# ScalarE issues the transfer of the rows of maxima itself, one transfer a half, in place of three on the sync engine

## The chip, the cores and the metric

The kernel runs on one core of one Trainium2 chip. The metric is device time in microseconds of one execution; the median of three runs is given. The profile is of one further execution. Engines are named TensorE (PE), VectorE (DVE), ScalarE (ACT), GpSimd (POOL) and the sync engine (SP), which only issues transfers.

## The reference

Two layers in sequence on `x` (16 sequences of 256 tokens, 256 features), each with a residual connection, both with 16 heads of 16 features:

```python
def layer0(x, t):                       # t: the condition, 16 x 64
    x1 = x + attention(tc_rmsnorm(x, t, g1, b1), Wq, Wk, Wv, Wo)      # softmax(q k / 4) v, no mask
    return x1 + swiglu(tc_rmsnorm(x1, t, g2, b2), gate_w, hid_w, out_w)   # hidden width 1024
x = x + layer0(x, cond_256)

def layer1(x, mask, c):
    scores = where(mask, -inf, q @ k.T / 4)          # one mask of 256 x 256 for all
    out = (softmax(scores) @ v) @ Wo.T
    xn = out / sqrt(mean(out * out) + 1e-6) * rms_scale
    shift, sc = split(silu(c) @ Wc.T + bc)
    return xn * (1 + sc) + shift
x = x + layer1(x, mask, cond_256)
```

The softmax needs the maximum of each row of scores. The kernel subtracts it by appending it, in three bf16 parts that add up to the f32 value, as three more rows of the operand that holds q (against rows of ones in the operand of k), so that a matmul gives scores minus maximum.

## The kernel before

The work is a pipeline over 32 sequence passes (16 sequences of layer 0, then 16 of layer 1). In step `s0` (from -3 to 33) each engine works on several passes at once: normalization of pass s+3 ("N"), q and k projections of s+2 ("A"), values and the first scores of s+1 ("V", "B1"), the second scores, exponentials and weighted sums of s ("B2"), the division and output projection of s-1 ("C"), and the feed-forward network of s-2 and s-3 ("C2", "C3") or the result of s-2 ("R"). Each step has eight slots `g`, one for two heads, and every engine's program is written out in its own order, slot by slot. Steps 3 to 12 and 19 to 28 are loops of two steps a turn, in which waits compare with registers. Nothing schedules: engines run their lists and meet at semaphores.

The maxima go through the engines twice in a step, once for each half of eight heads. TensorE's first scores (`s1ps`, L568 or L583) are reduced by VectorE to `nmax` (L875, L882); GpSimd splits them in three parts (`nparts`, L1247 to L1253); TensorE transposes the parts into a bank (`work` or `acc`, L726); ScalarE copies the bank to the buffer `rows`, 24 partitions by 256 (`shift_store`, L1092); SP moves `rows` into three partitions of the q operand `qst` (`rows_in`, L469). TensorE's second scores (`s2ps`, L606) of heads 0 and 8 wait for the landing (`shift_loaded`). The second half (heads 8 to 15) is handled in slot 1 of the step that uses it in slot 4; the first half is handled in slot 5 (from step 19 on at the head of slot 6 on ScalarE) and is used in slot 0 of the next step.

SP's list in a step: load x; `rows_in(1)`; write the parts `qp` of q and then `kp` of k to a scratch buffer in HBM (L412, two transfers each); after these have landed, `read_stack` of the first half (L422, three transfers of 384, 256 and 128 KB from scratch to the operands `stack`); in layer 1 store the result (L427); `rows_in(0)`; `read_stack` of the second half.

Names on ScalarE: `exps` (L1055, s2ps to `E`), `tanh` of feed-forward block i (L1073, bank F{i} to `th`), `h_high_part` (L1079, `hh`), `store_oT` (L1065), `query_high` (L1097) and the copy of k (L1146) that round the projections to bf16 in `qp` and `kp`, `middle` (L1102) that rounds VectorE's rest (L919) once more, and the copy `oh` (L1115), whose rest `ol` VectorE makes (L909) for the output projection on TensorE (L525 to L527 with `oh`, `ol`). `dg` (L945) are VectorE's diagonals of inverse roots, which TensorE broadcasts (L718). Two banks `work0`, `work1` are used in turn by all projections, so a bank is opened when its earlier use is read.

Of the kernel before, what the change touches and what calls it, by code (L numbers as in the profile page):

```python
# [58 lines left out]
MASKED = PARTS + 1  # L59
ROWS = MASKED + 3  # L60
SLOTS = 8
UNITS = 16
# [131 lines left out]
def after(eng, sem, count):  # L194

    if isinstance(count, int) and count <= 0:
        return
    eng.wait_ge(sem, count)
# [31 lines left out]
def build(nc, xT, w0, w_ffn, w_out, w1, condT, cond_w, cond_b, rms_scale, mask, maskT, yT):  # L230
    ctx = ExitStack()
    with ctx:
# [18 lines left out]
        qst = [t[:, 0, :, :] for t in stack]  # L251
# [36 lines left out]
        rows = sb("rows", [P, T], BF16)  # L288
# [94 lines left out]
        def _(sp):  # L383
# [53 lines left out]
            def step(st):  # L437
# [18 lines left out]

                rows_used = [held(UNITS * n_b2), held(UNITS * (n_b2 - 1))]
                rows_made = [None, None]
                for half_, stage in enumerate(("B1", "B2")):
                    if L[stage] is not None:  # L460
                        b, k = st.bank(f"sh{half_}")
                        rows_made[half_] = (work_free[b], held(k + 1))
                result_made = held(st.n(-2 - B) + 1)

                def rows_in(half_):
                    after(sp, s2_full, rows_used[half_])
                    after(sp, *rows_made[half_])
                    for r in range(3):
                        sp.dma_start(qst[par if half_ else 1 - par][MASKED + r:MASKED + r + 1, 8 * half_:8 * half_ + 8, :],  # L469
                                     rows[8 * r:8 * r + 8, :]).then_inc(shift_loaded[half_], 16)  # L470

# [14 lines left out]
                load_swap(4)  # L486
                if L["B2"] is not None:
                    rows_in(1)
                if L["A"] is not None:
# [13 lines left out]
                if L["R"] is not None:  # L503
                    store_result(st.n(-2 - B), result_made)
                if L["B1"] is not None:
                    rows_in(0)
                if L["A"] is not None:
# [12 lines left out]
        def _(pe):  # L520
# [67 lines left out]
            def scores(st, g):  # L588
                n, par = st.n(0), st.par
                if g in (0, 4):  # L590
                    after(pe, shift_loaded[g // 4], 48 * (n + 1))
                short = st.L["B2"] == 1 and not st.full
# [436 lines left out]
        def _(act):  # L1029
# [59 lines left out]
            def shift_store(st, half_):  # L1089
                bank, free = opened(st, f"sh{half_}")  # L1090
                after(act, shift_loaded[1 - half_], 48 * (st.n(0) + half_))
                a.copy(nT, bank[0:24, 0:P].bitcast(BF16)).then_inc(free, 1)  # L1092

            def query_high(st):
# [284 lines left out]
```

## Time and profile before

| | |
|---|---|
| median of 3 runs | 1008.09 us (1007.32 to 1013.06) |
| the profiled execution | 1008.46 us, of which the span from first to last instruction is 1006.6 us |
| mean granted TensorE clock | 0.967 of full |
| busy: PE, DVE, ACT, POOL | 90%, 57%, 54%, 41% |
| transfers | 91.29 MB, mean 91 GB/s |
| a steady step of layer 0 / of layer 1 | about 39.6 us / 17.4 us |

The span is 1.9 us shorter than the execution's own time. In the rows, an engine line gives start, duration, engine, line, operation, output and input, and in brackets the idle time just before it and what ended that; SPq is SP's queue, whose instructions are the issues and not the transfers' time. A queue can stand idle at no cost, and only what TensorE waits for reaches the end.

### The profile page before, as it was taken

Reading aid. Unit: us, or ns where it says so; the run is one execution under the profiler, and the core shown is the slowest. Engines: PE = TensorE matmul, PEld = TensorE weight load, DVE = VectorE, ACT = ScalarE, POOL = GpSimd, SP = SyncE. Lnnn points to the kernel's source line nnn. Section 1 sums busy time; section 2 is a strip of 40 time slices with the busy share of each in tenths; the row PEclk is TensorE's granted clock in tenths of the full one; section 3 lists DMA queues with packets and bytes.
Section 4 is the critical chain, followed back from the end, with each engine's and each line's share of the span. In section 5 each row is a group of like instructions: output and inputs, shape, how many; then the busy total and the mean of one; then the engine's idle time right before and its main releaser. Section 6 shows DMA issues by size and latency. Waiting matters only on the chain.

```text
span 1006.6 us, 24326 instructions
## 1 busy us (share of the span) xinstructions
PE 909.2 (90%) x8188; PEld 780.6 (78%) x8188; DVE 570.3 (57%) x1104; ACT 547.5 (54%) x1130; POOL 415.2 (41%) x633
## 2 busy tenths in 40 slices
PE   3578899999999999999999999999999789888874
PEld 3456698898888988988889889889887677777653
DVE  3366556557555565575565756545455455555541
ACT  2246556546455565464554665554556566666652
POOL 5223344443443444434334344344444454444522
PEclk9779999999999999999999999999999999999997
DMA  6555423322332233223322242232437576576611
GB/s 204 110 106 122 91 64 75 75 65 59 66 86 42 63 73 73 63 58 68 84 42 63 69 91 65 65 76 66 94 74 167 119 160 147 142 166 144 157 36 34
DMA packets 83070, 91.29 MB, mean 91 GB/s; under 512 B 7776, under 2 KB 70016, under 8 KB 83008
## 3 DMA queue, kind: packets, MB, share of 16 engines
q1 hardware_dynamic: 83008, 90.50, 39.8%
q8 instruction: 35, 0.57, 0.3%
q14 instruction: 27, 0.22, 0.1%
HBM read 60.30 MB, written 29.36 MB: 89 GB/s over the span
## 4 chain that ended last, share of the span: by engine, by line
PE 73%; issue 8%; DVE 7%; ACT 5%; POOL 3%; DMA 1%; SPq 1%; POOLq 0%; DVEq 0%; ACTq 0%
PE work L525 11%; PE work L527 11%; PE work L526 11%; PE pvps L622 8%; PE s2ps L606 7%; PE s1ps L583 5%; PE work L710 4%; PE acc L525 3%; PE acc L526 2%; PE acc L527 2%; PE work L656 2%; PE s1ps L568 2%; PE work L718 1%; DVE rest L919 1%; DVE th L959 1%
## 5 line engine op out<-in xcount | busy, mean ns | idle before, releaser
L1055 ACT ACTIVATE E<-s2ps 128x512 f32<-128x512 f32 x384 | 214.1, 596 | 184.2 <-PE s2ps L606 110.8
L882 DVE TENSOR_REDUCE nmax<-s1ps 128x2 f32<-128x512 f32 x256 | 163.9, 682 | 32.1 <-PE s1ps L583 31.9
L525 PE MATMUL work<-xch,Gh 128*128 128x256 f32 x512 | 154.5, 302 | 0.0
L959 DVE SCALAR_TENSOR_TENSOR th<-th,work 128x256 f32<-128x256 f32 x128 | 53.8, 420 | 168.7 <-ACT th L1073 168.7
L1328 POOL TENSOR_TENSOR hl<-hf,hh 128x256 fp32r<-128x256 f32 x128 | 94.9, 742 | 131.0 <-PE acc L527 77.3
L526 PE MATMUL work<-xcl,Gh 128*128 128x256 f32 x512 | 147.1, 287 | 0.0
L527 PE MATMUL work<-xch,Gl 128*128 128x256 f32 x512 | 146.9, 287 | 0.0
L606 PE MATMUL s2ps<-stack 100*128 100x256 bf16 x768 | 127.7, 275 | 2.1 <-DMA stack<-rows 2.0
L875 DVE TENSOR_REDUCE nmax<-s1ps 128x4 f32<-128x512 f32 x128 | 85.6, 685 | 36.5 <-PE s1ps L568 36.4
L525 PEld LDWEIGHTS work<-xch,Gh 128*128 128x128 f32 x512 | 99.3, 194 | 8.2 <-issue 6.6
L622 PE MATMUL pvps<-E,vaug 128*32 128x256 f32 x1536 | 97.5, 387 | 6.3 <-ACT E L1055 4.0
L1233 POOL TENSOR_TENSOR qp<-rest,qp 128x512 bf16<-128x512 f32 x32 | 37.2, 1163 | 156.3 <-ACT qp L1102 156.3
L527 PEld LDWEIGHTS work<-xch,Gl 128*128 128x128 f32 x512 | 100.0, 195 | 0.0
L526 PEld LDWEIGHTS work<-xcl,Gh 128*128 128x128 f32 x512 | 99.9, 195 | 0.0
L583 PE MATMUL s1ps<-stack 96*128 96x256 bf16 x512 | 81.9, 281 | 9.4 <-DMA stack<-scr 4.9
L1073 ACT ACTIVATE th<-work 128x256 f32<-128x256 f32 x128 | 49.1, 384 | 72.3 <-PE work L527 72.3
L525 PE MATMUL work<-xnh,Wh 128*128 128x256 f32 x256 | 79.3, 310 | 1.4 <-issue 0.8
L606 PEld LDWEIGHTS s2ps<-stack 100*128 100x128 bf16 x768 | 67.3, 98 | 14.1 <-issue 2.3
L622 PEld LDWEIGHTS pvps<-E,vaug 128*32 128x32 f32 x1536 | 43.8, 110 | 40.3 <-issue 9.5
L525 PE MATMUL acc<-hh,Uh 128*128 128x256 f32 x256 | 74.2, 290 | 0.2
L526 PE MATMUL work<-xnl,Wh 128*128 128x256 f32 x256 | 74.4, 291 | 0.0
L527 PE MATMUL work<-xnh,Wl 128*128 128x256 f32 x256 | 74.2, 290 | 0.0
(131 smaller groups left out, 2149.1 us busy)
## 6 DMA issues: line engine op xcount, KB each, us to landing
stack<-scr SPq DMA_DIRECT2D x64, 384.0 KB, 4.6
stack<-scr SPq DMA_DIRECT2D x64, 256.0 KB, 5.2
scr<-qp SPq DMA_DIRECT2D x64, 192.0 KB, 2.3
scr<-kp SPq DMA_DIRECT2D x64, 192.0 KB, 2.3
stack<-scr SPq DMA_DIRECT2D x64, 128.0 KB, 5.6
X<-xT SPq DMA_DIRECT2D x16, 256.0 KB, 4.5
yT<-crm SPq DMA_DIRECT2D x16, 256.0 KB, 5.2
stack<-rows SPq DMA_DIRECT2D x196, 4.0 KB
```

The source lines that it names most:

```text
L525: mm(out, lh, rh, start=first, stop=False, skip_group_check=True)
L526: mm(out, lh, rl, start=False, stop=False, skip_group_check=True)
L527: return mm(out, ll, rh, start=False, stop=last, skip_group_check=True)
L583: last = mm(bank[:, T * i:T * (i + 1)], qst[par][0:PARTS, h, P * qh:P * (qh + 1)], kst[par][0:PARTS, h, :], start=st.L["B1"] == 0, stop=Tr ...
L606: last = mm(bank[:, T * i:T * (i + 1)], kst[par][0:ROWS, h, P * kh:P * (kh + 1)], qst[par][0:ROWS, h, :], start=not add_mask, stop=True, s ...
L622: last = mm(pvps[32 * i:32 * (i + 1), T * (j % 2):T * (j % 2 + 1)], v_of[:, kh, h, :], E[:, exp_slot(layer, st.full, h // 2, kh), T * (h % ...
L875: v.tensor_reduce(nmax[:, g // 4, :, 2 * (g % 4):2 * (g % 4) + 2], s1ps[g % 2][:, :].rearrange("p (q h t) -> p q h t", q=2, h=2), AX_X, AL ...
L882: v.tensor_reduce(nmax[:, g // 4, qh, 2 * (g % 4):2 * (g % 4) + 2], s1ps[u % 2][:, :].rearrange("p (h t) -> p h t", h=2), AX_X, ALU.max, n ...
L959: v.scalar_tensor_tensor(th[:, i % 2, :], th[:, i % 2, :], 1.0, bank[:, 0:T], ALU.add, ALU.mult).then_inc(silu_ready, 1)
L1055: a.activation(E[:, exp_slot(st.L["B2"], st.full, g, kh), :], s2ps[g % 2 if short else u % 2][:, :], ACT.Exp, scale=SCORE_SCALE).then_inc( ...
L1073: a.activation(th[:, i % 2, :], bank[:, 0:T], ACT.Tanh, scale=0.5).then_inc(tanh_ready, 1)
L1328: p.tensor_tensor(hl[:, i % 2, :], hf[:, i % 2, :], hh[:, i % 2, :].bitcast(F32), ALU.subtract).then_inc(h_low, 1)
```

## The change

`rows_in` and its counts leave SP's program. ScalarE's `shift_store` now issues one transfer from the 24 partitions of `rows` to all three partitions of `qst`, behind its own copy: it waits that the scores which last used those heads are done (`s2_full`) and that its own copy is done (`work_free[b]`). The semaphore `shift_loaded` then counts 16 a half in place of 48, and the two waits on it, on TensorE and on ScalarE, follow. Layer, data and all other orders stay.

```diff
--- before.py
+++ after.py
@@ -454,20 +454,7 @@
-                rows_used = [held(UNITS * n_b2), held(UNITS * (n_b2 - 1))]
-                rows_made = [None, None]
-                for half_, stage in enumerate(("B1", "B2")):
-                    if L[stage] is not None:
-                        b, k = st.bank(f"sh{half_}")
-                        rows_made[half_] = (work_free[b], held(k + 1))
                 result_made = held(st.n(-2 - B) + 1)
-
-                def rows_in(half_):
-                    after(sp, s2_full, rows_used[half_])
-                    after(sp, *rows_made[half_])
-                    for r in range(3):
-                        sp.dma_start(qst[par if half_ else 1 - par][MASKED + r:MASKED + r + 1, 8 * half_:8 * half_ + 8, :],
-                                     rows[8 * r:8 * r + 8, :]).then_inc(shift_loaded[half_], 16)
@@ -484,8 +471,6 @@
-                if L["B2"] is not None:
-                    rows_in(1)
@@ -502,8 +487,6 @@
-                if L["B1"] is not None:
-                    rows_in(0)
@@ -588,7 +571,7 @@
-                    after(pe, shift_loaded[g // 4], 48 * (n + 1))
+                    after(pe, shift_loaded[g // 4], 16 * (n + 1))
@@ -1088,8 +1071,14 @@
                 bank, free = opened(st, f"sh{half_}")
-                after(act, shift_loaded[1 - half_], 48 * (st.n(0) + half_))
+                after(act, shift_loaded[1 - half_], 16 * (st.n(0) + half_))
                 a.copy(nT, bank[0:24, 0:P].bitcast(BF16)).then_inc(free, 1)
+
+                b, k = st.bank(f"sh{half_}")
+                after(act, s2_full, UNITS * (st.n(0) - half_))
+                after(act, work_free[b], k + 1)
+                act.dma_start(qst[st.par if half_ else 1 - st.par][MASKED:ROWS, 8 * half_:8 * half_ + 8, :],
+                              nT).then_inc(shift_loaded[half_], 16)
```

ScalarE's list in slot 5 of a layer 0 step (`rows` is the copy of the maxima, `th` the tanh of block 5, `hh` the cast of block 4's h; the names in brackets are the semaphores that the instruction waits for). Before:

```order
88 L1065 COPY oT<-pvps 128x512 [waits work_full1,work_full0,pv_done]
89 L1092 COPY rows<-work 24x256 [waits shift_loaded1,work_full1]
90 L1073 ACTIVATE th<-work 128x256 [waits work_free0,work_full0]
91 L1079 CAST hh<-hf 128x256 [waits down_done,work_free1]
92 L1055 ACTIVATE E<-s2ps 128x512 [waits pv_done,s2_full] x2
```

And in the changed kernel:

```order
94 L1048 COPY oT<-pvps 128x512 [waits work_full1,work_full0,pv_done]
95 L1075 COPY rows<-work 24x256 [waits shift_loaded1,work_full1]
96 L1080 DMA stack<-rows 3x8x256 [waits work_free1,s2_full]
97 L1056 ACTIVATE th<-work 128x256 [waits work_free0,work_full0]
98 L1062 CAST hh<-hf 128x256 [waits down_done,work_free1]
99 L1038 ACTIVATE E<-s2ps 128x512 [waits pv_done,s2_full] x2
```

One issue stands between the copy and the tanh; nothing else moved.

ScalarE's list in slot 1 of a layer 1 step (`kp` first the copy and then the middle part of k). Before:

```order
519 L1092 COPY rows<-acc 24x256 [waits shift_loaded0]
520 L198 REGISTER_ALU
521 L1146 CAST kp<-work 128x512 [waits k_written,work_full1]
522 L1102 CAST kp<-rest 128x512 [waits work_free1]
523 L198 REGISTER_ALU
```

And in the changed kernel:

```order
542 L1075 COPY rows<-acc 24x256 [waits shift_loaded0]
543 L198 REGISTER_ALU
544 L1080 DMA stack<-rows 3x8x256 [waits work_free2,s2_full]
545 L198 REGISTER_ALU
546 L1135 CAST kp<-work 128x512 [waits k_written,work_full1]
547 L1091 CAST kp<-rest 128x512 [waits work_free1]
```

Here the issue and one more register operation stand ahead of k's copy. SP's list loses its three transfers a half, 32 steps long, and keeps its other transfers in their order.

## Rows read from the trace of the kernel before

**Rows 1.** The page, its first part: busy time of each engine.

```profile
PE 909.2 (90%) x8188; PEld 780.6 (78%) x8188; DVE 570.3 (57%) x1104; ACT 547.5 (54%) x1130; POOL 415.2 (41%) x633
```

**Rows 2.** Waits of SP's queue: total us, times, longest.

```profile
SPq L198 <- ACT rows L1092: 349.3, 59, 10.6
```

**Rows 3.** Issues on SP: minimum, median and maximum duration in ns.

```profile
L469 SPq DMA_DIRECT2D stack<-rows x192: 634/640/794, 60.0 to 977.8; - x192
...
L422 SPq DMA_DIRECT2D stack<-scr x192: 308/427/1412, 38.2 to 955.1; - x192
```

**Rows 4.** TensorE's waits from 690 to 985 us, which holds layer 1.

```profile
PE work L525 <- DVE ol L909: 19.1, 13, 1.6
...
PE s2ps L606 <- DMA stack<-rows: 2.0, 3, 1.5
```

**Rows 5.** Timeline of one layer 1 step, SP's issues and TensorE.

```profile
791.96 2.07 SPq L469 DMA_DIRECT2D stack<-rows  x3
...
796.57 0.40 PE L568 MATMUL s1ps<-stack 97*128 97x128 bf16 x4 [1.24 <-DMA stack<-scr]
...
798.44 0.39 PE L606 MATMUL s2ps<-stack 100*128 100x256 bf16 x2 [1.48 <-DMA stack<-rows]
```

**Rows 6.** Timeline of slots 5 and 6 of a layer 0 step.

```profile
387.87 0.36 ACT L1092 COPY rows<-work 24x256 bf16<-24x256 bf16 x1
388.13 0.38 ACT L1073 ACTIVATE th<-work 128x256 f32<-128x256 f32 x1
...
388.54 0.42 DVE L959 SCALAR_TENSOR_TENSOR th<-th,work 128x256 f32<-128x256 f32 x1 [1.26 <-ACT th L1073]
...
390.53 0.68 DVE L945 TENSOR_TENSOR dg<-ident,rstd 128x512 f32<-128x512 f32 x1
...
391.54 0.42 DVE L959 SCALAR_TENSOR_TENSOR th<-th,work 128x256 f32<-128x256 f32 x1 [0.33 <-ACT th L1073]
391.64 0.60 PE L718 MATMUL work<-dg,ones 128*128 128x256 f32 x2
...
392.47 0.70 PE L718 MATMUL work<-dg,ones 128*128 128x256 f32 x2 [0.23 <-DVE hf L963]
```

**Rows 7.** Timeline of slots 1 to 3 of a layer 1 step.

```profile
834.80 1.16 POOL L1233 TENSOR_TENSOR qp<-rest,qp 128x512 bf16<-128x512 f32 x1 [2.08 <-ACT qp L1102]
...
836.03 0.34 ACT L1092 COPY rows<-acc 24x256 bf16<-24x256 bf16 x1
...
836.45 2.02 SPq L469 DMA_DIRECT2D stack<-rows  x3
...
836.93 0.59 ACT L1146 CAST kp<-work 128x512 bf16<-128x512 f32 x1 [0.55 <-PE work L527]
...
839.47 0.69 DVE L909 TENSOR_TENSOR ol<-work,oh 128x512 fp32r<-128x512 f32 x1 [1.17 <-ACT oh L1115]
...
840.21 0.39 PE L525 MATMUL work<-oh,Wh 128*128 128x256 f32 x1 [1.56 <-DVE ol L909]
```

**Rows 8.** Timeline, what stands behind the copy of the rows in other steps.

```profile
267.38 0.38 ACT L1073 ACTIVATE th<-work 128x256 f32<-128x256 f32 x1 [1.00 <-PE work L527]
...
365.76 0.59 ACT L1097 CAST qp<-work 128x512 bf16<-128x512 f32 x1 [0.41 <-PE work L527]
...
592.20 0.41 DVE L945 TENSOR_TENSOR dg<-ident,rstd 128x256 f32<-128x256 f32 x1
593.25 0.60 PE L718 MATMUL work<-dg,ones 128*128 128x256 f32 x2
...
764.29 0.59 ACT L1146 CAST kp<-work 128x512 bf16<-128x512 f32 x1 [0.55 <-PE work L527]
...
847.47 1.09 ACT L1055 ACTIVATE E<-s2ps 128x512 f32<-128x512 f32 x2 [1.06 <-PE s2ps L606]
```

**Rows 9.** Chain of waits, ScalarE's queue between two instructions: start, us, what.

```profile
838.54 0.06 issue
838.60 0.04 ACTq L198
```

## The prediction

> **What bounds the kernel now.** I read the page first. TensorE is busy 90% of the span and the other engines 41% to 57% [rows 1], so a transfer or a wait counts only where TensorE stands behind it. The waits of SP's queue come next, because the change is made there: SP stands 349.3 us at the rows of maxima [rows 2]. That figure is no price. It is idle time of a queue, and I ask who waits for SP. TensorE's own waits answer: over the whole of layer 1 it lost 2.0 us in three waits to the landed rows, against 19.1 us in thirteen waits to the low half of the attention output (`ol`) [rows 4]. So the removed stand is nearly free already, and the question is what the step costs on ScalarE, where the 19.1 us chain begins.
>
> **What is removed.** Per half SP issues three transfers; 192 of them lasted 640 ns each at the median [rows 3], so SP gets back 192 x 0.64 = 123 us of issuing. What stands behind them on SP: behind the second half's rows, the writes of qp; behind the first half's, the second half of the stack load. In layer 0 the qp write waits for GpSimd anyway, and the stack load for TensorE's scores. In layer 1 the write of qp could start some 2.5 us earlier (GpSimd has the low part ready at 834.80 + 1.16 = 835.96, while SP is still to issue until 838.5), but the stack load needs kp as well, whose write is issued after GpSimd's later kp part [rows 7]. So the stack load does not move: 0. The second half's load moves up by under 1 us and is wanted half a step later: 0.
>
> What can be gained is the late landing. In one step the rows were issued at 791.96, behind the first half of the stack and the result's store on SP's queue, and TensorE waited 1.48 us for them at 798.44, after 1.24 us for the stack itself [rows 5]. The other two waits of the kind make up 0.5 us. A transfer issued by ScalarE starts earlier and does not stand in SP's queue. I count all three waits, 2.0 us [rows 4], as gained, and leave the 1.24 us.
>
> At this place the Trainium skill speaks both ways. "DMA: Bandwidth & Descriptors", section "Queues, rings and completion order", says that a DMA engine takes turns between the queue rows that have work, packet by packet, so the rows on ScalarE's own row would pass the backlog; by that, 2.0 us come back, as I count. Its section "Issuing engines are not separate DMA queues" says that transfers of all engines interleave on the same sixteen engines and that only issuing time is saved; by that the waits would partly stay and the sum be up to 2 us higher. No row of before has a transfer on ScalarE's queue.
>
> **What is added: 64 issues on ScalarE.** Each stands behind ScalarE's own copy (0.34 to 0.36 us [rows 6, 7]) and must see it finished, where the next instruction now starts while the copy still drains. No row shows an issue on ScalarE. The nearest rows are SP's: 640 ns for one row of the same data, 427 ns for a stack transfer of up to 384 KB [rows 3]. The time does not follow bytes or pieces, so I take 0.64 us for the one transfer of three rows, with 0.43 below, zero as the far lower end, and three times 0.65 = 1.95 us as the upper end, if it costs what its three parts did. Around it: 0.08 us from the copy's end to the issue (836.03 + 0.34 to SP's issue at 836.45 [rows 7]) and about 0.2 us for two queued waits of the next instruction, at 0.06 + 0.04 us each [rows 9].
>
> The Trainium skill has a price that would make all this vanish: "DMA: Bandwidth & Descriptors", section "Anatomy of one DMA", lists about 50 ns for a sequencer's dispatch. The 640 ns rows of SP contradict it for the issuing queue, and I go by the rows; with 50 ns the sum would be the gain alone, 1006.1.
>
> *Layer 0, slot 5.* Here `tanh` of block 5 stands directly behind the copy of the rows: copy at 387.87, tanh at 388.13 [rows 6]. Now: copy ends 388.23, + 0.08 + 0.64 + 0.2 = 389.15, 1.02 us later. VectorE's product starts from it at 388.54 and runs without idle time through two maxima to the diagonals, which end at 390.53 + 0.68 = 391.21; TensorE takes them at 391.64 [rows 6]. Of the 0.43 us between, 0.06 is the signal; 0.37 us is cover. 1.02 - 0.37 = 0.65 us come through. The second broadcast at 392.47 moves as much, because VectorE's next product (391.54, idle 0.33 before it) falls behind the diagonals. Six steps of the trace look so (their copies start at 147, 187, 226, 348, 388 and 427 us; the fifth stands for them): 6 x 0.65 = 3.9. Two more, the one shown and the next, have shorter diagonals: 592.20 + 0.41 = 592.61 against 593.25 leaves 0.58 of cover, 0.44 come through [rows 8], 0.9 together. In the other loop steps TensorE reaches the place later and tanh already waits 1.0 us for it [rows 8]: 0. The cast of h behind the tanh moves along; GpSimd and the down projection that read it come late enough by my reading: 0.
>
> *Layer 0, slot 1.* The next instruction, the copy of qp, waits 0.41 us for TensorE now [rows 8] and would start about 0.5 us later. The bank that it shares with VectorE is wanted again after about that time: I take 0, and 0.1 us in each of 13 steps as the bound.
>
> *Layer 1, slot 1.* The rows' copy ends at 836.37. kp's copy starts at 836.93, when TensorE is through [rows 7]. Now 836.37 + 0.08 + 0.64 + 0.2 = 837.29, so 0.36 us late, and everything behind it is the chain at which TensorE waits: kp's rest on VectorE, its middle part and `oh` on ScalarE, `ol` on VectorE (839.47), TensorE at 840.21 after 1.56 us idle [rows 7]. No cover at all. Eleven steps look so, the first at 764.29 [rows 8], the last at 942.59: 11 x 0.36 = 4.0.
>
> *Layer 1, slot 6.* The exponentials behind the copy wait 1.06 us for TensorE [rows 8]; 0.08 + 0.64 + 0.2 = 0.92 fits: 0.
>
> **Sum.** 3.9 + 0.9 + 4.0 - 2.0 = +6.8 us on the profiled 1008.46, which lies 0.4 above the median of 1008.09: 1014.9 on the median. I take **1015.0**. With 0.43 us an issue: 6 x 0.44 + 2 x 0.23 + 11 x 0.15 - 2.0 = +2.8, 1010.8; with 0.85 us, +10.8, 1018.9. Every other cost of ScalarE's is between zero and (c) below.
>
> **Rivals.**
> (a) *The issue is nearly free on ScalarE.* At up to 0.2 us all covers hold and the gain of 2.0 us is left: 1006. For it: nothing on ScalarE was measured. Against: SP's rows never fall below 308 ns.
> (b) *Two issuers collide (slower).* SP no longer stands at the rows, so in layer 1 it issues the two qp writes at about 836.03 and holds until 836.95, exactly when ScalarE wants to issue (836.45). If one must wait for the other, kp's chain loses 0.5 us more: 11 x 0.5 = 5.5, together 1020.4. It decides where SP's pair begins before ScalarE's copy ends, in every step of that kind. Against: layer 0 has the two apart. The Trainium skill's "Perfetto Trace Analysis", section on the HWDGE DMA instruction, describes a lock that an issuer waits for, on a descriptor generator shared by two sequencers; no run here shows it yet.
> (c) *One transfer costs what its three parts did.* With 1.95 us, each term grows by 1.31: 6 x 1.96 + 2 x 1.75 + 11 x 1.67 - 2.0 = +31.6, 1039.7, and slot 6 of layer 1 loses its cover too. Against: the stack rows, whose many pieces cost 427 ns.
> (d) *More is gained than the waits show.* The step of rows 5 may be late because of SP's queue as a whole, and its 1.24 us go too; with a free issue as in (a) that is 1008.1 - 2.0 - 1.2 = 1004.9, and any shorter standing in eleven steps may add a little: about 1003. A gain of over 1% has no row.
>
> **How the numbers follow.** Forecast 0.50, (a) 0.20, (b) 0.17, (c) 0.06, (d) 0.07. One per cent, 10 us, is about what a measurement of this kernel tells from no change. The forecast with its bounds spans 1010.8 to 1018.9. The range reaches over (a) and (b), with room in (b) for a somewhat longer issue: 1004 to 1025. Slower by over 1% (above 1018.2): all of (c), nearly all of (b) and the top of the forecast, 0.29. Faster by over 1%: 0.06. Within: 0.65.
>
> **What will show it.** ScalarE's queue has 64 issues; their length decides nearly all. In layer 0's slot 5 the tanh starts about 1.3 us behind the start of the rows' copy instead of 0.26, and TensorE gets a new wait for the diagonals, about 0.6 us, six times. In layer 1 the wait for `ol` grows from 1.6 to 1.9 us, and the waits for landed rows go. SP's longest waits turn to GpSimd's qp. I am wrong if the issue on ScalarE is not near 0.64 us, if SP's issues and ScalarE's stretch one another, or if the intervals of lower granted clock in layer 0, each worth more than a microsecond, fall on other slots.

## The result and the profile after

The changed kernel took 1032.79 us (median of 4 runs, 1030.51 to 1034.88) against 1010.58 us (4 runs, 1007.32 to 1014.01) for the kernel before on the same chip: ratio 1.0194, 95% interval [1.0158, 1.0229]. It is slower, and 8 us above the upper end of the range. The profiled execution took 1030.51 us, its span is 1028.6 us, the granted clock 0.954 of full speed on average. The line numbers of the changed kernel are 17 lower on TensorE, VectorE and in most of ScalarE's code (L508 for L525, L892 for L909, L1075 for L1092) and 11 lower for what stands behind the issue in the program (L1135 for L1146, L1086 for L1097, L1222 for L1233). The issue on ScalarE is L1080.

The page of the changed kernel, busy time of each engine (against [rows 1]):

```profile
PE 923.3 (90%) x8188; PEld 788.1 (77%) x8188; DVE 572.3 (56%) x1104; ACT 547.3 (53%) x1130; POOL 416.1 (40%) x633
```

The same 8188 matmuls kept TensorE busy 14.1 us longer, and its idle time (span less busy) went from 1006.6 - 909.2 = 97.4 to 1028.6 - 923.3 = 105.3 us. So 8 us of the difference between the two profiles are waits and 14 us are matmuls that ran slower.

The issues on ScalarE: minimum, median and maximum in ns, first and last start.

```profile
L1080 ACTq DMA_DIRECT2D stack<-rows x64: 728/733/1346, 58.0 to 997.4; - x64
```

Timeline of the changed kernel, slots 5 and 6 of a layer 0 step (against [rows 6]):

```profile
192.25 0.36 ACT L1075 COPY rows<-work 24x256 bf16<-24x256 bf16 x1
192.70 0.73 ACTq L1080 DMA_DIRECT2D stack<-rows  x1
193.60 0.38 ACT L1056 ACTIVATE th<-work 128x256 f32<-128x256 f32 x1 [0.99 <-ACT rows L1075]
...
196.84 1.40 PE L701 MATMUL work<-dg,ones 128*128 128x256 f32 x4 [0.65 <-DVE dg L928]
```

From the copy's end (192.61) to the issue are 0.09 us, the issue takes 0.73, and 0.17 us behind it the tanh starts: 1.35 us behind the start of the copy, where it was 0.26. TensorE has a wait for the diagonals that was not there, 0.65 us.

Slot 1 of layer 0 (against the 0.41 us in [rows 8]), and slot 1 of layer 1 with the chain behind it (against [rows 7]), both from the timeline:

```profile
169.15 0.35 ACT L1075 COPY rows<-work 24x256 bf16<-24x256 bf16 x1
169.59 0.77 ACTq L1080 DMA_DIRECT2D stack<-rows  x1
170.47 0.58 ACT L1086 CAST qp<-work 128x512 bf16<-128x512 f32 x1 [0.97 <-PE work L510]
...
855.57 0.35 ACT L1075 COPY rows<-acc 24x256 bf16<-24x256 bf16 x1
856.00 0.73 ACTq L1080 DMA_DIRECT2D stack<-rows  x1
856.89 0.58 ACT L1135 CAST kp<-work 128x512 bf16<-128x512 f32 x1 [0.98 <-PE work L510]
...
859.42 0.69 DVE L892 TENSOR_TENSOR ol<-work,oh 128x512 fp32r<-128x512 f32 x1 [1.17 <-ACT oh L1104]
860.17 0.39 PE L508 MATMUL work<-oh,Wh 128*128 128x256 f32 x1 [1.98 <-DVE ol L892]
```

The name behind the arrow can mislead: k's copy "waits 0.98 us for PE", but what ran out last is ScalarE's own issue, 856.00 + 0.73 = 856.73. The copy of k starts 1.32 us behind the start of the copy of the rows, against 0.90 before, and TensorE waits 1.98 instead of 1.56 us.

Waits of the changed kernel, TensorE and then SP's queue (us in total, times, longest; in the kernel before, over the whole program, `ol` had 20.6 us in 14, the diagonals 15.6 us in 5):

```profile
PE work L508 <- DVE ol L892: 25.2, 14, 2.1
PE work L701 <- DVE dg L928: 20.1, 13, 5.7
...
PE s2ps L589 <- DMA stack<-rows: 3.4, 3, 2.2
```

```profile
SPq L422 <- PE s2ps L589: 269.5, 28, 17.0
SPq L198 <- POOL qp L1222: 235.7, 26, 15.9
```

SP's stand at the rows [rows 2] is gone and turned into others, as forecast. But the waits for landed rows did not go: 3.4 us against 2.0 [rows 4]. The longest stands where layer 1's maxima meet the first full pair of stack loads:

```profile
771.46 0.73 ACTq L1080 DMA_DIRECT2D stack<-rows  x1
...
771.69 1.48 SPq L422 DMA_DIRECT2D stack<-scr  x3
...
777.13 0.39 PE L589 MATMUL s2ps<-stack 100*128 100x256 bf16 x2 [2.21 <-DMA stack<-rows]
```

SP no longer stands at the rows, so it issues the second half of the stack load (768 KB) 0.23 us behind the start of ScalarE's issue. In the trace's record of packets the 24 packets of the rows begin at 774.56, 3.1 us behind the start of the issue, and end at 775.44; TensorE goes on at 777.1. In the kernel before the three transfers of the rows were issued at 757.50 to 759.51, ahead of the stack load at 759.55, and TensorE waited 0.27 us at 760.76.

**Where the time went, by stretches.** The borders are starts of the same copies of the rows in both kernels; columns: stretch, its length, busy time of the engines (with counts of instructions), granted clock, share of the DMA engines, GB/s. Before:

```profile
0.00:124.45 124.45, 81.74 (x588) 62.54 (x589) 65.19 (x114) 52.77 (x91) 46.03 (x71) 0.89 0.54 128
124.45:589.47 465.02, 458.80 (x4114) 409.98 (x4113) 284.63 (x540) 253.35 (x556) 192.97 (x278) 0.98 0.31 67
589.47:757.07 167.60, 163.95 (x1524) 146.22 (x1523) 91.99 (x191) 92.69 (x204) 71.53 (x109) 1.00 0.34 76
757.07:773.41 16.34, 14.23 (x144) 11.32 (x142) 9.68 (x19) 11.51 (x24) 7.44 (x14) 1.00 0.67 149
773.41:951.67 178.26, 155.38 (x1543) 125.97 (x1542) 100.12 (x200) 114.95 (x220) 83.48 (x140) 0.99 0.66 149
951.67:1006.60 54.93, 35.15 (x286) 24.61 (x285) 18.68 (x40) 22.20 (x43) 13.79 (x23) 0.83 0.19 48
```

After:

```profile
0.00:128.68 128.68, 86.92 (x588) 64.34 (x589) 66.49 (x114) 53.07 (x91) 46.01 (x71) 0.83 0.51 124
128.68:600.72 472.04, 462.35 (x4114) 410.88 (x4113) 285.35 (x540) 253.84 (x556) 194.40 (x278) 0.98 0.29 66
600.72:771.01 170.29, 165.25 (x1524) 146.58 (x1523) 91.78 (x191) 92.53 (x205) 71.47 (x109) 1.00 0.33 75
771.01:791.54 20.53, 15.77 (x143) 12.51 (x142) 9.87 (x19) 11.39 (x24) 7.33 (x14) 0.92 0.50 113
791.54:975.09 183.55, 159.39 (x1543) 130.44 (x1543) 100.11 (x200) 114.40 (x221) 83.14 (x140) 0.96 0.64 145
975.09:1028.60 53.51, 33.60 (x286) 23.37 (x285) 18.69 (x40) 22.09 (x43) 13.71 (x23) 0.85 0.20 49
```

Longer by 4.2 us at the start, 7.0 in layer 0, 2.7 on the way to layer 1, 4.2 in the one step of the late landing, 5.3 in layer 1, and 1.4 shorter at the end: 22.0. At the start TensorE does not wait longer (124.45 - 81.74 = 42.7 us idle before, 41.8 after); the same 588 matmuls take 86.92 instead of 81.74 us, at a clock of 0.83 instead of 0.89. In layer 1 the granted clock is 0.96 against 0.99. In detail, three equal stretches of one step of the changed kernel:

```profile
838.80:842.20 3.40, 1.34 (x13) 1.06 (x11) 2.16 (x4) 1.84 (x4) 1.16 (x1) 1.00 0.07 19
842.20:845.60 3.40, 3.40 (x19) 3.40 (x17) 0.95 (x3) 1.93 (x4) 2.35 (x3) 0.51 0.58 158
845.60:849.00 3.40, 3.40 (x42) 2.22 (x42) 1.38 (x2) 2.90 (x6) 1.96 (x5) 0.99 1.03 190
```

In the first TensorE is idle 2.06 us, waiting for `ol`; in the second it is busy throughout at half the clock (0.51, which is 1.2 of 2.4 GHz) and gets 19 matmuls begun, against 42 in the third.

**The base moved too.** The kernel before was run again beside the experiments. 74 of these runs have a median of 1013.9 us (1005.7 to 1023.5), with granted clocks of 0.946 to 0.967; time and clock go together (correlation -0.8). Two more, of 1062.9 and 2187.1 us, lie far outside and are left out here and below. The 1008.09 us and the profile that I started from, at 0.967, are the fast edge of that. So the change costs 17 to 19 us of 1014 (16.8 us on the one chip where both kernels were run again), and the 14 us of slower matmuls between the two profiles are in part this luck.

### The profile page after: what moved, and what is told of

The parts are those of the page before. It is cut to its first block, busy times and chain, and to the rows that moved or that the text cites. A ratio compares the mean times of both kernels' runs of the same rounds, so it can differ in the third digit from the quotient of the medians.

```text
span 1028.6 us, 24173 instructions
## 1 busy us (share of the span) xinstructions
PE 923.3 (90%) x8188; PEld 788.1 (77%) x8188; DVE 572.3 (56%) x1104; ACT 547.3 (53%) x1130; POOL 416.1 (40%) x633
## 4 chain that ended last, share of the span: by engine, by line
PE 64%; issue 12%; DVE 8%; ACT 7%; POOL 4%; ACTq 2%; DMA 2%; POOLq 0%; SPq 0%; DVEq 0%
PE work L508 10%; PE work L509 9%; PE work L510 9%; PE pvps L605 8%; PE s2ps L589 6%; PE s1ps L566 5%; PE work L693 4%; PE work L639 2%; PE acc L508 2%; PE work L701 2%; PE acc L509 2%; PE acc L510 2%; ACTq L1080 2%; DVE nmax L865 2%; DMA stack<-rows 1%
## 5 line engine op out<-in xcount | busy, mean ns | idle before, releaser
L508 PE MATMUL work<-xch,Gh 128*128 128x256 f32 x512 | 155.1, 303 | 0.1
L508 PEld LDWEIGHTS work<-xch,Gh 128*128 128x128 f32 x512 | 99.8, 195 | 8.5 <-issue 6.6
L1222 POOL TENSOR_TENSOR qp<-rest,qp 128x512 bf16<-128x512 f32 x32 | 37.1, 1160 | 158.8 <-ACT qp L1091 158.8
L508 PE MATMUL work<-xnh,Wh 128*128 128x256 f32 x256 | 79.2, 309 | 1.8 <-issue 0.7
L1222 POOL TENSOR_TENSOR kp<-rest,kp 128x512 bf16<-128x512 f32 x32 | 37.2, 1161 | 95.5 <-ACT kp L1091 95.5
L508 PE MATMUL acc<-hh,Uh 128*128 128x256 f32 x256 | 73.9, 289 | 0.3
```

The source lines that it names most:

```text
L508: mm(out, lh, rh, start=first, stop=False, skip_group_check=True)
L1222: p.tensor_tensor(parts[:, lo_at, :, :], rest[:, :, :], parts[:, 1, :, :], ALU.subtract).then_inc(low, 1)
```

## The experiments

TensorE's idle time is span less busy time of the profiled execution. The kernel before had medians of 1014.2 us beside `sp_one`, the two halves and `act_late` (one chip), 1014.4 us beside `act_pad`, `changed_again` and the first two fillings (a second chip), and on a third chip 1012.6 us beside `act_wait`, `act_from3`, `act_three` and `sp_one_fill` and 1013.3 us beside the two holds and `act_fill0`. Times from different chips are best compared by their distance from these. What is called an interval of lower clock below is a short stretch in which TensorE runs at about half its clock.

### One transfer, still on SP

```diff
-                    for r in range(3):
-                        sp.dma_start(qst[par if half_ else 1 - par][MASKED + r:MASKED + r + 1, 8 * half_:8 * half_ + 8, :],
-                                     rows[8 * r:8 * r + 8, :]).then_inc(shift_loaded[half_], 16)
+                    sp.dma_start(qst[par if half_ else 1 - par][MASKED:ROWS, 8 * half_:8 * half_ + 8, :],
+                                 nT).then_inc(shift_loaded[half_], 16)
```

> The kernel before, but SP issues the three rows as one transfer (24 partitions to 3) in its old places; ScalarE issues nothing. Theory A (the cost is ScalarE's issue: 0.73 us and the wait for its own copy, 64 times, ahead of work that TensorE waits for, and the lower granted clock that follows TensorE's longer idle times): as before within 0.4%, no new wait of TensorE for the diagonals, wait for ol at 1.6 us, SP gets back 1.3 us a half. Theory B (the merged transfer lands later than three small ones): slower than before by 0.3% or more, with waits for stack<-rows at the 3.4 us of the changed kernel or above.

1010.76 us, ratio 0.9973 [0.9946, 0.9999]; TensorE idle 91.6 us. Waits of TensorE, and the issue in the timeline at the switch to layer 1:

```profile
PE work L524 <- DVE ol L908: 20.2, 14, 1.6
PE work L717 <- DVE dg L944: 14.6, 5, 5.7
...
PE s2ps L605 <- DMA stack<-rows: 0.6, 1, 0.6
```

```profile
762.53 0.73 SPq L468 DMA_DIRECT2D stack<-rows  x1
763.30 1.36 SPq L422 DMA_DIRECT2D stack<-scr  x3
```

The gain that I counted exists, 1.4 of the 2.0 us of waits for rows and nearly 6 us of idle time in all, but it belongs to the one transfer in place of three, not to the engine that issues it. And one transfer of three rows costs SP 0.73 us too: ScalarE issues neither faster nor slower.

### ScalarE issues one half only

Two kernels, on the base of the last: `act_half1` leaves the first half to SP and gives the second (slot 1) to ScalarE, `act_half0` the other way (slots 5 and 6).

```diff
                 a.copy(nT, bank[0:24, 0:P].bitcast(BF16)).then_inc(free, 1)
+                if not (half_ == 1):
+                    return
+                b, k = st.bank(f"sh{half_}")
+                after(act, s2_full, UNITS * (st.n(0) - half_))
+                after(act, work_free[b], k + 1)
+                act.dma_start(qst[st.par if half_ else 1 - st.par][MASKED:ROWS, 8 * half_:8 * half_ + 8, :],
+                              nT).then_inc(shift_loaded[half_], 16)
```

> Half of the change: ScalarE issues only the second half's rows (slot 1), SP the first half's as one transfer. Theory A: the wait for ol grows from 1.6 to about 2.0 us in eleven steps of layer 1 (+4.5 us) and TensorE is at half clock in some three or four more intervals there (+5 to 7 us); no new wait for the diagonals in layer 0. In all +7 to +14 us. Theory B (landing): under +3 us, because the second half's landing is not waited for.

> The other half of the change: ScalarE issues only the first half's rows (slot 5, slot 6 from step 19), SP the second half's as one transfer. Theory A: the new wait for the diagonals, 0.65 us in some seven steps of layer 0 and 0.4 in two more (+5 us), the wait for ol stays at 1.6 us, in all +5 to +10 us. Theory B: all of the change's loss (+20 us) is here, with waits for stack<-rows of 3 us or more in layer 1.

`act_half1`: 1013.12 us, ratio 0.9981 [0.9947, 1.0014], 2.4 us over the single transfer on SP, less than expected. Its waits are as expected, `ol` at 25.4 us, and its idle time is 98.4 us, 6.8 more; but its ten runs had the higher clock, 0.964 on average against 0.955. The stretches tell where, though no experiment tells why: between the copies that stand at 124.45 and 589.47 us in the kernel before (layer 0), `act_half1` took 461.60 us at a clock of 1.00 and the single transfer on SP 468.01 us at 0.97, while in layer 1 (773.41 to 951.67) it took 184.09 against 177.04 us. So layer 1 lost 7 us, the lower end of what was expected, and a layer 0 faster by 6.4 us hid most of it.

`act_half0`: 1023.3 us, ratio 1.0093 [1.0064, 1.0121], 12.5 us over it, a little more than expected. TensorE's waits:

```profile
PE work L717 <- DVE dg L944: 18.2, 10, 5.7
...
PE s2ps L605 <- DMA stack<-rows: 2.4, 1, 2.4
```

The new waits for diagonals and the late landing belong to the first half, the longer `ol` to the second.

### The issues at places where ScalarE waits anyway

The changed kernel with the issue in a function of its own, called later: the first half behind the cast of h in slot 6 (layer 1: as now), the second behind the exponentials of slot 3 (from step 19: 2).

```diff
+                    if g == (2 if st.s0 >= SPARE else 3) and L["B2"] is not None:
+                        shift_issue(st, 1)
...
+                    if g == 6 and st.s0 < SPARE and L["B1"] is not None:
+                        shift_issue(st, 0)
```

> ScalarE issues both halves' transfers as in the changed kernel, but at places where it stood idle in the trace: the first half's behind the cast of h in slot 6 (steps before 19) and as now in slot 6 (from step 19), the second half's behind the exponentials of slot 3 (slot 2 from step 19). Theory A: the loss goes, within 4 us of the kernel before; no wait for the diagonals, wait for ol at 1.6 us. Theory B or a theory that SP's freed queue disturbs the loads: as slow as the changed kernel, +15 us or more.

1017.53 us, ratio 1.0021 [0.9986, 1.0055], 3.3 us over the kernel before. `ol` is back at 20.6 us and the diagonals at 14.0, but TensorE waits 5.0 us in five waits for landed rows, the longest here in the timeline:

```profile
767.83 0.73 ACTq L1081 DMA_DIRECT2D stack<-rows  x1
768.07 1.47 SPq L422 DMA_DIRECT2D stack<-scr  x3
...
773.36 0.39 PE L589 MATMUL s2ps<-stack 100*128 100x256 bf16 x2 [2.53 <-DMA stack<-rows]
```

Sixty-four issues of 0.73 us on ScalarE cost nearly nothing where nobody waits behind them. The place is the price, not the issue.

### ScalarE held without a transfer

The kernel before; behind ScalarE's copy come the change's two waits and two copies that nobody reads.

```diff
+                for r in range(2):
+                    after(act, pad_done, 2 * (2 * st.n(0) + 2 - half_) + r)
+                    a.copy(rows[64:88, :].rearrange("p (r t) -> p r t", r=2),
+                           ones[64:88, :][:, None, :].to_broadcast([24, 2, P])).then_inc(pad_done, 1)
```

> The kernel before, with SP's three transfers as they were; ScalarE only gets, behind its copy of the rows, the two waits of the change and then two small copies in a row, which together hold it about as long as the issue did (estimated from the 0.26 us between two such instructions and the 0.36 us of one: about 0.7 to 0.8 us), and which nobody reads. It parts the time that ScalarE is held from the transfer itself. Theory A (the loss is ScalarE being held in front of tanh in layer 0 and in front of k's copy in layer 1, with the lower granted clock that follows): TensorE gets waits for the diagonals of about 0.6 us in six or seven steps of layer 0 and the wait for ol grows from 1.6 to about 2.0 us, though no transfer is on ScalarE's queue; the time is +12 to +22 us over before. Rival B (the transfer issued by ScalarE is what costs: later landing, descriptor work, another queue): the same waits would appear but the time stays within 6 us of before.

The changed kernel once more, as the base on this chip:

> The changed kernel once more, on the same chip as the next experiments, as their base. Both theories: 1.5 to 2.3% over before.

The two copies took 0.83 us together and the tanh of slot 5 started 1.38 us behind the copy of the rows (191.77, 193.15), as long as in the changed kernel. The padded kernel took 1028.81 us, ratio 1.0138 [1.0055, 1.0221], the changed one 1031.16 us, 1.0145 [1.0062, 1.0228]. Waits of the padded kernel:

```profile
PE work L526 <- DVE ol L910: 25.7, 14, 2.1
PE work L719 <- DVE dg L946: 21.6, 15, 5.7
```

Its idle time is 106.3 us against 105.9 in the changed kernel. So 14.5 of 16.8 us come without any transfer on ScalarE's queue; rival B falls. The other 2.3 us are not clear of the spread of four runs.

### ScalarE only waits

> The kernel before; ScalarE gets only the two waits of the change behind its copy of the rows (own copy done, scores done), and neither issue nor padding. SP keeps its transfers. By the rows the tanh of layer 0 then starts about 0.3 us later than before, which is less than the 0.37 us of cover in front of the diagonals, and k's copy of layer 1 (0.55 us of idle time in front of it) not later at all. Theory A: no new waits for diagonals, ol stays at 1.6 us, and the time is within 3 us of before. Rival B (to see its own copy finished is itself dear on ScalarE): 4 us and more over before.

```diff
+                b, k = st.bank(f"sh{half_}")
+                after(act, s2_full, UNITS * (st.n(0) - half_))
+                after(act, work_free[b], k + 1)
```

1015.54 us, ratio 1.0023 [0.9991, 1.0054], 2.9 us over the kernel before and not clear of it; `ol` 20.9 us in 14, diagonals 15.1 us in 5, idle 95.5 us. The tanh of slot 5 starts 0.59 us behind the start of the copy instead of 0.26 (189.53, 190.12). The cover of [rows 6], which is the slack between the diagonals' end and TensorE's use of them, takes the 0.3 us, as worked out.

### Matmuls that fill TensorE's wait

Twelve matmuls ahead of layer 1's output projection, into the bank that it overwrites, in the changed kernel (`act_fill`) and in the kernel before (`sp_fill`).

```diff
             def output_projection(st):
+                if st.s0 >= SPARE:
+                    bank, full = open_bank(st, "Wo")
+                    for _i in range(12):
+                        mm(bank[:, 0:D], Wh[:, 3, 0, 0:P], Wl[:, 3, 0, :], start=True, stop=True, skip_group_check=True)
```

> The changed kernel, and in layer 1 (from step 19) TensorE runs twelve matmuls of 128x256 ahead of the output projection into the bank that this will fill from its start, while it waits for ol; their result is overwritten. Theory A (the intervals of lower granted clock in layer 1 follow TensorE's idle time of about 2 us at ol): the intervals at 777, 804, 842, 896 and 951 us thin out to two or fewer, TensorE's busy time outside the added matmuls falls by several us, and the time is 3 to 8 us under the changed kernel, if the added matmuls fit into the wait. Rival B (the clock falls regardless of this idle time): as many intervals as before, and the time is the same or, where the matmuls outlast the wait, up to 5 us longer.

> The kernel before with the same twelve matmuls in front of the output projection in layer 1. Theory A: its wait there was 1.6 us, and only about two intervals of lower clock stood in layer 1, so 0 to 3 us faster than before. Rival B: unchanged, or up to 5 us slower since twelve matmuls may outlast a wait of 1.6 us.

`act_fill` took 1026.81 us, 4.3 us under the changed kernel on the same chip, although it does more work. Its timeline, and the stretch that answers to 791.54:975.09 above:

```profile
854.41 1.69 PE L673 MATMUL work<-Wl,Wh 128*128 128x256 f32 x12
...
856.27 0.39 PE L508 MATMUL work<-oh,Wh 128*128 128x256 f32 x1 [0.18 <-DVE ol L896]
```

```profile
790.41:968.97 178.56, 170.91 (x1663) 139.60 (x1663) 100.12 (x200) 114.53 (x221) 83.26 (x140) 1.00 0.66 148
```

`ol` comes no earlier, at 855.53, 3.87 us behind the start of the copy of the rows at 851.66 (without the filling 859.42 - 855.57 = 3.85), yet the stretch is 178.56 instead of 183.55 us, at a clock of 1.00 instead of 0.96. Here the clock followed TensorE's idle time (7.7 instead of 24.2 us in the stretch). `sp_fill` took 1011.73 us, 2.6 us under the kernel before, ratio 0.996 [0.9923, 0.9997], with a clock of 1.00 in layer 1 as well; it had less to win, as expected.

The same in layer 0, five matmuls ahead of the first broadcast of slot 6:

> The changed kernel, and in layer 0 from step 3 on TensorE runs five matmuls of 128x256 ahead of the first broadcast of slot 6, into the bank that this overwrites, while it waits 0.65 us for the diagonals. Theory A (what the change lost in layer 0 between 147 and 589 us is idle time alone, since both kernels have five intervals of lower clock there): as many intervals as without them and the time within 2 us of the changed kernel, since the diagonals come no earlier. Rival B (there too the clock follows the new idle time, as in layer 1): intervals go, and it is 2 to 6 us faster than the changed kernel.

1030.50 us, 0.7 under the changed kernel of the other chip, ratio 1.0171 [1.0117, 1.0225]. The diagonals' waits of 0.65 us are filled (17.4 us in 6 against 21.5 in 13), its profile has three intervals of lower clock in layer 0 where the changed kernel had five, and the time is the same within what can be told. In layer 0 the filling wins nothing: the diagonals come no earlier, and what they delay stays delayed. Idle time alone does not set the clock: in the layer 0 stretch named above, the single transfer on SP has 6.2 us of idle time at a clock of 0.97, and `act_half1` 7.0 us at 1.00.

### The first steps left to SP

```diff
+                if not (st.s0 >= 3):
+                    return
```

with SP's single transfer in steps below 3.

> The changed kernel, but in the first steps (up to step 2) SP still issues the one transfer a half; ScalarE issues from step 3 on. Between the kernels the copies of the rows had shifted by 4.6 us at 147 us already, which my sum has no term for. Theory A (that part comes from ScalarE being held in the start-up steps, where TensorE waits for it as well): 3 to 6 us under the changed kernel, about 1026. Rival B (the 4.6 us are the clock at the start, which varies from one execution to the next): within 2 us of the changed kernel.

1028.18 us, 3.0 under `changed_again` and 4.6 under the first measurement, on other chips; against the kernel before on its own chip it loses 15.6 us where `changed_again` loses 16.8, so the times tell nothing sure. In the trace the copy that stands at 124.45 us before starts at 124.29, where the changed kernel had 128.68. But this trace is of the fastest of the four runs, and kernels whose ScalarE issues nothing differ as much:

```profile
0.00:124.29 124.29, 81.79 (x588) 62.57 (x589) 65.55 (x114) 52.75 (x91) 45.95 (x71) 0.89 0.54 128
...
0.00:127.16 127.16, 86.63 (x588) 64.86 (x589) 66.43 (x114) 53.20 (x90) 46.05 (x71) 0.84 0.53 125
```

The first line is `act_from3`, the second `act_wait`. The same copy starts at 124.3 to 127.2 us in the six traces without an issue on ScalarE in the first steps (mean 125.6) and at 126.9 to 130.0 in the five with the whole change (mean 128.4). So rival B, the clock at the start, explains much of this, and a start-up part of the change is likely, 2.8 us by the means, but not shown. Whatever it is, it is matmuls at the lower clock and not waiting.

### Three transfers on ScalarE

The issue in a loop of three, one for each part.

> The changed kernel, but ScalarE issues three transfers a half, as SP did, so that it is held for three times 0.73 = 2.2 us instead of 0.73 us. Theory A (held time goes through once the cover is used up): 1.46 us more in some ten steps of layer 0 and eleven of layer 1, 31 us, and up to 10 us more at places that had cover until now: 30 to 45 us over the changed kernel, 1060 to 1075. Rival B (a fixed price for having the transfer on ScalarE's queue): under 10 us over the changed kernel.

1152.52 us, ratio 1.1371 [1.1327, 1.1416]: 121 us over the changed kernel (on another chip), three times the expected. One issue of one row is 627 ns, the three of a half hold ScalarE 1.96 us. TensorE is busy 979.2 us, 56 more, and idle 178.6, 73 more; its clock is 0.902. Its waits:

```profile
PE work L508 <- DVE ol L892: 36.4, 13, 3.3
PE work L701 <- DVE dg L928: 28.3, 18, 6.5
PE work L653 <- DVE rest L902: 21.1, 17, 1.9
PE s2ps L589 <- DMA stack<-rows: 17.1, 12, 3.0
```

Theory A had the direction and not the shape: the cost is no line through the two places where cover ran out. With 1.2 us more in a row, waits open that had none (k's rest, landed rows in twelve steps), and each longer idle time is followed by slower matmuls. My rival (c) worked out 1039.7 us for this hold with the same straight line.

### SP holds the stack load back until the rows have landed

```diff
+                rows_landed = held(16 * (n_b1 + 1))
...
+                    if L["B1"] is not None:
+                        after(sp, shift_loaded[0], rows_landed)
                     mask_row_in(st, 1)
                     read_stack(par, 1)
```

In the changed kernel (`stack_hold`) and in the one with late issues (`late_hold`).

> The changed kernel, and SP waits ahead of the second half of the stack load until ScalarE's transfer of the first half's rows has landed (it stood at their issue in the kernel before). Theory A (SP, no longer standing at the rows, issues the stack load in the same moment as ScalarE its rows, and the rows land behind it: issue at 771.46, stack load at 771.69, TensorE waits 2.21 us and a lower clock follows): the wait for landed rows in the step where layer 1's first scores begin goes from 2.2 us to under 0.5 us, its jump of 3.8 us between the copies of 757 and 763 us goes, and the time is 3 to 4 us under the changed kernel, about 1028. Rival B (a transfer on ScalarE's queue lands late by itself): the wait stays at about 2 us and the time within 2 us of the changed kernel.

> The kernel whose ScalarE issues later, at places where it waits anyway (1017.53 us, with 5.0 us of waits for landed rows), with the same hold on SP. Theory A: it loses most of those 5.0 us and comes to 1012 to 1014 us, level with the kernel before. Rival B: unchanged at 1017.

`stack_hold`: 1026.81 us, ratio 1.0138 [1.0084, 1.0191]. That is 4.4 us under the changed kernel on another chip, and by the distance from the kernel before 3.3 us (13.5 against 16.8). Its timeline:

```profile
771.48 0.73 ACTq L1083 DMA_DIRECT2D stack<-rows  x1
...
773.72 1.25 SPq L422 DMA_DIRECT2D stack<-scr  x3
```

No wait for landed rows is left on TensorE in layer 1, and from this copy to the next it takes 6.7 us, nearly as before (6.33), where the changed kernel took 10.1: 3.4 us in this one step. The rows issued at 771.48 were home by 773.7; their packets ran from 772.85 to 773.11, 1.4 us behind the start of the issue and not 3.1, and took 0.3 instead of 0.9 us. `late_hold`: 1012.78 us, ratio 1.0009 [0.9976, 1.0042], 4.7 less than without the hold (on another chip; 3.8 by the distances from the kernel before), and its waits for rows fell from 5.0 us in five to 1.5 us in three. So a transfer on ScalarE's queue does not land late by itself; it does when the stack load is issued beside it. In `sp_one` the rows, issued by SP 0.77 us ahead of the same load, have their first packet 1.4 us behind the issue as well (763.90). Whether a lead of 0.23 us would be enough on SP's own queue was not tried.

### The two good parts together

SP's single transfer, and the twelve matmuls.

> SP issues one transfer a half in the old places, and TensorE has the twelve matmuls ahead of the output projection in layer 1. The single transfer had a ratio of 0.997 to before and the matmuls one of 0.996. Theory A (both independent): 0.993, 1005 to 1008 us. Rival B (both were the spread of the kernel before): within 0.2% of before.

1008.66 us, ratio 0.9952 [0.9932, 0.9971]: faster than both kernels, by half a per cent over the one before, with the issues where they always were. It is a little less than the two gains together (0.993).

## Why the prediction was wrong

**Right**: what bounds the kernel and where ScalarE's 64 issues meet it. The places were the two named, the tanh of slot 5 and k's copy in slot 1 of layer 1, and `act_wait`, `act_pad` and `act_late` show that time held at these places is the cause. The terms around the issue were 0.09 and 0.17 us for 0.08 and 0.2. Layer 0's slot 5 was forecast at 6 x 0.65 + 2 x 0.44; the trace has six new waits of 0.65 in the loop's steps and two of about 0.4 behind them. That it is six again is partly luck: they stand at 156, 197, 279, 361, 443 and 524 us, in the 1st, 2nd, 4th, 6th, 8th and 10th of these steps, and the forecast named the 1st to 3rd and 6th to 8th. In the others TensorE comes late from an interval of lower clock; both traces have five of these, in different steps. Layer 1's slot 1 was forecast at 11 x 0.36 = 4.0; the copy of k is 0.42 us later and the waits for `ol` grew by 22.7 - 19.1 = 3.6 us in the window of [rows 4] and 4.6 us over the whole program. Two issuers did not collide (rival b): ScalarE's issue took 0.73 us beside SP's pair at 855.58, the same as alone, and 0.73 to 0.75 in all eleven places from 760 us on where they overlap. The figure of about 50 ns that the prediction quotes from the Trainium skill, "DMA: Bandwidth & Descriptors", section "Anatomy of one DMA", stands there for the path of transfers issued by GpSimd, so it was no price for this issue, and 0.73 us does not contradict it.

**A size**: 0.64 us for an issue measured 0.73. The rule that time doesn't follow the pieces was taken a little too far: one row takes 0.63 to 0.64 us on either engine, three rows 0.73.

**The step that failed first** is "the second half's load moves up by under 1 us and is wanted half a step later: 0", and with it "I count all three waits, 2.0 us [rows 4], as gained". I asked who needs the stack load and not what it runs over. SP's stand was what kept 768 KB behind the rows; without it they went out together, the waits grew to 3.4 us and the clock fell behind the longest of them. The step in `stack_hold` prices this at 3.4 us. The 2.0 us could be had, but from the single transfer on SP.

**Terms that were missing.** These weigh as much. The first steps: I counted from the copy at 147 us on, and 4.6 us had been lost by then between the two profiles; 2.8 us of it is what the means above leave for the change, and that is not shown. Slot 1 of layer 0: "I take 0, and 0.1 us in each of 13 steps as the bound"; from the copy of slot 1 to that of slot 5 each of some eleven steps is 0.2 us longer than before (169.15 to 192.25 is 23.10 us; 163.93 to 186.82 was 22.89), which `act_half1` shows as well and `act_half0` does not: 2.2 us. And the clock: it had no term in the sum; I named it among what could make the forecast wrong, but for layer 0, and it was layer 1 that lost by it, where `act_fill` gave 4.3 us back. Since `sp_fill` gave 2.6 us back in the kernel before, only the difference, some 2 us, belongs to the change.

**The base**: 5.8 us of the miss are none of the change's. By steps: 1008.1 + 5.8 (median of the 74 runs) + 6.8 (my sum) + 3.4 (order of the transfers) + 2.8 (first steps) + 2.2 (slot 1) = 1029.1, against 1031.2 and 1032.8 measured. The padded kernel gives a second division of the 16.8 us: 14.5 for holding ScalarE, where my three terms for it were 8.8, and 2.3 for everything that comes with the transfer, where I had a gain of 2.0. So the held time was 5.7 us short and the landing 4.3. Each of these carries about 2 us of uncertainty, and the clock's part is inside them, so the last 2 to 4 us are not worth a story.

**Open**: why the kernels' clocks differ where their idle times don't (`act_half1` has 98.4 us of idle time and 0.964, the single transfer on SP 91.6 us and 0.955), and what holds ScalarE's rows back beside the stack load. It is not the issue, which took 0.73 us with and without it; 1.7 us more pass between the issue and the first packet, 0.6 us more among the packets, and about 1 us more behind the last of them.

## What to carry to other kernels

An issue on a compute engine costs its full time (here 0.73 us) of that engine, so put it where the engine waits anyway; right behind the producer it costs most of its time wherever the next instruction feeds the bound. When a queue stops standing at something, ask what it will now issue earlier, and which transfer that overtakes or runs beside. And take the base from many runs with their clocks before a sum of a few microseconds is laid on it: an added wait on TensorE costs its length and then, in some steps, slower matmuls behind it.

## What the runs showed of the hardware

- The issue takes the same on SP and ScalarE: 0.73 us for three rows of 4 KB in one transfer, 0.63 to 0.64 us for one row. It did not stretch when both issued within the same 0.9 us. Two of the 64 issues took 1.3 us, one of them with no issue on SP beside it.
- A transfer of 12 KB on ScalarE's own queue row, issued 0.23 us ahead of 768 KB on SP's, let its reader start 5.7 us after its issue began (771.46 to 777.13); with the 768 KB held back until it had landed, these went out 2.2 us after it (771.48 to 773.72). I had read the rule of turns between queue rows (the Trainium skill, "DMA: Bandwidth & Descriptors", section "Queues, rings and completion order") as a promise that a small transfer passes a large one; this trace doesn't bear that out. It fits the same page's section "Issuing engines are not separate DMA queues" in the Trainium skill: transfers of all issuing engines run on the same sixteen DMA engines and interleave there.
- TensorE's granted clock fell to 0.51 in a stretch that followed 2.06 us of waiting, and it stayed at 1.00 over the stretch of layer 1 when those waits were filled with matmuls whose results nobody reads: 183.55 us became 178.56. Filling waits of 0.65 us in layer 0 changed no time.
